# Layer 2 of a four-layer kernel: the second transposes of every odd unit move to the PSUM bank of the query products

## The reference

```
q = z @ wq @ fcq_w + fcq_b            # 16 heads of 64, likewise k and v
scores = einsum('bihd,bjhd->bhij', q, k) / scale
attn = softmax(scores, axis=-1)
out = einsum('bhij,bjhd->bihd', attn, v)
return out.reshape(b, n, 1024) @ fco_w + fco_b
```

## Time and profile before

| | us |
|---|---|
| median of three timed executions | 2760.54 |
| the profiled execution | 2755.35 |
| its span, first to last instruction | 2753.6 |
| layer 2, slots of the attention | about 1339 to 2074 |
| TensorE busy over the span | 2410.3 |
| idle of TensorE before the transposes of L2143 | 69.2 |

### The profile page before, as it was taken

How to read it: one execution, slowest core, us unless ns; L and a number is a source line. 1 busy time by engine, 2 the same in 40 slices (tenths; PEclk the granted TensorE clock), 3 DMA queues, 4 the chain that set the end, 5 groups by cost and what they waited for, 6 DMA issues and landing times.

```text
span 2753.6 us, 39485 instructions
## 1 busy us (share of the span) xinstructions
PE 2410.3 (88%) x13864; PEld 1554.8 (56%) x13864; DVE 1810.2 (66%) x3844; ACT 1306.5 (47%) x3393; POOL 1239.2 (45%) x1120
## 2 busy tenths in 40 slices
PE   6687799999999999997888999999889689897888
PEld 3475345555555555555445666665554467676766
DVE  5677576777767777664678777777656664656634
ACT  4576524344343433433355666666546324445443
POOL 2553166676776777763366333332000541333331
PEclk8899799999999999997899999999999787999999
DMA  4464300000000000002912222222101262212113
GB/s 171 143 196 137 97 1 1 1 1 1 1 1 1 1 1 1 1 1 92 222 41 66 69 71 70 70 70 77 32 1 36 60 184 50 57 44 57 34 51 100
DMA packets 189333, 158.82 MB, mean 58 GB/s; under 512 B 101408, under 2 KB 168480, under 8 KB 188320
## 3 DMA queue, kind: packets, MB, share of 16 engines
q1 hardware_dynamic: 166352, 90.25, 12.1%
q0 software_dynamic: 22784, 66.05, 7.8%
HBM read 126.49 MB, written 59.51 MB: 68 GB/s over the span
## 4 chain that ended last, share of the span: by engine, by line
PE 38%; DVE 9%; ACT 4%; issue 2%; DMA 0%; POOL 0%; SPq 0%; ACTq 0%; DVEq 0%
PE bank L65 32%; PE bank L2143 4%; DVE work L2151 2%; DVE work L2087 2%; ACT work L2113 1%; ACT L3341 1%; DVE weights_odd L3455 1%; DVE weights_odd L3457 0%; DVE work L3403 0%; ACT weights_odd L3067 0%; DVE work L2131 0%; DVE weights_even L3403 0%; DVE work L3606 0%; PE bank L3014 0%; DVE work L3455 0%
## 5 line engine op out<-in xcount | busy, mean ns | idle before, releaser
L1535 POOL TENSOR_TENSOR work<-work 128x512 f32<-128x512 f32 x384 | 489.0, 1273 | 302.3 <-DVE work L1527 282.4
L65 PE MATMUL bank<-work 64*128 64x256 f32 (+5 forms) x4384 | 589.3, 352 | 26.2 <-ACT work L3381 8.0
L65 PE MATMUL bank<-weights_odd,normed_channels 128*128 128x512 f32 (+2 forms) x1088 | 509.8, 576 | 53.1 <-DVE work L1527 52.5
L65 PEld LDWEIGHTS bank<-work 64*128 64x128 f32 (+4 forms) x4384 | 412.0, 171 | 228.9 <-issue 151.4
L2113 ACT ACTIVATE work<-bank,work 128x256 f32<-128x256 f32 x512 | 235.9, 473 | 243.3 <-DVE work L2100 238.5
L1527 DVE TENSOR_TENSOR work<-bank,work 128x512 f32<-128x512 f32 x360 | 244.7, 687 | 113.1 <-PE bank L65 101.8
L65 PEld LDWEIGHTS bank<-weights_odd,normed_channels 128*128 128x128 f32 x1088 | 175.9, 193 | 180.0 <-DVE work L1527 99.4
L1602 ACT ACTIVATE work<-bank,work 128x256 f32<-128x256 f32 x256 | 119.0, 470 | 297.1 <-DVE work L1589 296.9
L599 POOL DMA_INDIRECT weights_even<-in_L_Wx,expert_slots x112 | 113.4, 1012 | 291.4 <-PE bank L672 224.9
L2087 DVE TENSOR_REDUCE work<-bank 128x2 f32<-128x512 f32 x256 | 164.8, 685 | 119.6 <-PE bank L65 119.3
L2143 PE MATMUL bank<-constants,work 128*128 128x128 f32 x1024 | 164.9, 284 | 69.2 <-DVE work L2151 64.2
(11 more groups left out here) (355 smaller groups left out, 4211.8 us busy)
## 6 DMA issues: line engine op xcount, KB each, us to landing
filter_matrices<-in_L_filters SPq DMA_DIRECT2D x24, 512.0 KB, 7.6
work<-filter_matrices SPq DMA_DIRECT2D x16, 768.0 KB, 5.7
weights_even<-noted_rows SPq DMA_DIRECT2D x56, 132.0 KB, 2.3
noted_rows<-in_empty SPq DMA_DIRECT2D x11, 660.0 KB, 9.4
noted_rows_in<-in_empty SPq DMA_DIRECT2D x8, 660.0 KB, 9.2
weights_odd<-noted_rows_in SPq DMA_DIRECT2D x40, 132.0 KB, 2.2
work<-token_rows SPq DMA_DIRECT2D x16, 256.0 KB, 3.5
token_rows_out<-in_zeros SPq DMA_DIRECT2D x6, 640.0 KB, 19.0
```

The costliest lines, as they stand in the source:

```text
L65: return pe.matmul(out, lhsT, rhs, start=first, stop=last, skip_group_check=True)
L1535: gp.tensor_tensor(self.sum_of(p), self.sum_of(p), self.product_of(p), ALU.add).then_inc(s["l1_add"], 1)
```

## The change

The second transposes of every odd unit, and their evacuation by ScalarE, use the bank `b_misc`. Their wait on VectorE's copy of half 0 goes; in its place comes a wait for the evacuation of the latest query product. The query product waits until ScalarE has read the transposes from `b_misc`. The first transposes of an even unit wait for VectorE's copy of half 0 of the unit before, no longer for ScalarE's copy of half 1.

```
     def tensor_query(self, pe, on, n):
         s, (g, m) = self.k.sem, divmod(n, L2_PAIRS)
         on.wait_ge(s["l2_q"], n)
+        self.wait_turned_scores(on, 2 * (2 * n - 5) + 1)
         mm(pe, self.b_misc[:, :], self.Fq[:, m * P:(m + 1) * P], cols(self.k.xn, g)).then_inc(s["l2_q_mm"], 1)
...
+    def turn_bank(self, n, half):
+
+        return self.b_misc if half == 1 and n % 2 == 1 else self.b_turn
+
     def tensor_turn(self, pe, on, n, half):
-        s, h = self.k.sem, 2 * n + half
+        s, h, bank = self.k.sem, 2 * n + half, self.turn_bank(n, half)
         on.wait_ge(s["l2_p"], 2 * h + 2)
-        self.wait_turned_scores(on, h - 1)
+        if half == 1 and n % 2 == 1:
+            on.wait_ge(s["l2_q"], min((n + 5) // 2, L2_PAIRS * GROUPS))
+        elif half == 1:
+            self.wait_turned_scores(on, h - 1)
+        else:
+            self.wait_turned_scores(on, 2 * (n - 1) + (n % 2 == 1))
         for jc in range(2):
             for i in range(2):
-                last = pe.transpose(self.b_turn[:, jc * SEQ + i * P:jc * SEQ + (i + 1) * P],
+                last = pe.transpose(bank[:, jc * SEQ + i * P:jc * SEQ + (i + 1) * P],
                                     self.p[h % 6][:, i * SEQ + jc * P:i * SEQ + (jc + 1) * P], self.k.ident)
         last.then_inc(s["l2_pt_mm"], 1)
...
         on.wait_ge(s["l2_pv"], n - 1)
-        a.activation(self.pt[h % 4], self.b_turn[:, :], ACT.Copy).then_inc(s["l2_pt_act"], 1)
+        a.activation(self.pt[h % 4], self.turn_bank(n, 1)[:, :], ACT.Copy).then_inc(s["l2_pt_act"], 1)
```

## The result

The changed kernel takes 2717.2 us (median of 4 runs, 2709.2 to 2717.9) against 2761.5 us (median of 4, 2758.0 to 2763.7): a ratio of 0.983, 95% interval 0.982 to 0.985. That is 44.3 us less; forecast were 50.5 us less and 2710.0. The same kernel, timed again on two later occasions, gave 0.982 [0.980, 0.984] (2708.3 against 2760.7 us, 52.4 less) and 0.982 [0.978, 0.986] (2790.9 against 2843.1 us, 52.1 less). The kernel before itself took 2761 us on two of the four occasions and 2843 and 2839 us on the other two, so kernels are compared within one occasion, or stage by stage.

A forecast was written before the change was run, and what follows sets the result against it. The prediction took TensorE to set the pace among the expert pairs. Its terms, 33.8 + 6.5 + 3.9 + 3.7 + 4.3 - 1.7 = 50.5 us, came off 2760.54 for 2710.0 us; range 2698 to 2728.

The forecast's parts named there:

- The wait and its price: Odd second transposes: without the wait for VectorE's copy, 0.93 us less per pair of slots, 33.8 us over 36 expert pairs.
- The floor in plain slots: Eight pairs without experts or staging: VectorE and ScalarE become the bound, gain 0.43 to 0.51 us each, 3.9 in sum.
- The first slots: First five odd slots with VectorE busy routing: shorter waits at separate places, 4.3 us gained in sum.
- part (c): Even first transposes wait for a copy that ended long before: frees 2.1 us at most, taken at 0.
- Behind the experts: Slots behind the expert pairs: 6.2 us gained, 3.7 in slots with joins and 2.5 in plain pairs.
- The rows of the first pair: Slot 32: TensorE arrives before the fetched rows, whose time GpSimd's scatters set; 1.7 us given back, bounds 0 and 4.
- The added waits: Query waits for ScalarE's copy, odd half 1 for the query's evacuation with 3.3 us of cover: both cost 0.
- Nothing behind layer 2 depends on a clock of its own, so the rest moves as a block: Everything after layer 2: shifts earlier unchanged, giving 2704.9 us profiled and 2710.0 us for the median.
- Rival 1: All slots: VectorE and ScalarE bind at 0.5 us; expert pairs lose 15.5 us of gain, 2725.5 us; chance 0.12.
- rival 2: All slots: no floor, the whole 64.2 us wait for VectorE's copy comes off, 2696.3 us; chance 0.12.
- rival 3: New waits end as late as the old, or the gain is lost elsewhere: 2760 us, give or take 3; chance 0.05.
- Rival 4: Expert pairs: TensorE's clock falls to 1.2 GHz, a quarter of them giving 2801 us; chance 0.03.

The follow-up runs named there:

- e1: Changed kernel with the odd second transposes waiting again for VectorE's copy of half 0: 2845.5 us against 2843.1 for the kernel before, ratio 1.0015.
- e6: Changed kernel plus one more VectorE maximum (128x256) in every unit of layer 2: ratio 0.984 to the kernel before, layer 2 685.0 us.
- e7: Changed kernel with TensorE issuing the four second transposes of every odd unit twice: ratio 0.988 to the kernel before, layer 2 701.7 us.
- e5: Changed kernel with first transposes of even units also waiting for ScalarE's copy again: ratio 0.981 to the kernel before, layer 2 678.3 us.
- e8: Changed kernel unedited, timed and profiled again: ratio 0.982 to the kernel before, layer 2 680.3 us, layer 3 683.2 us.
- e9: Changed kernel with expert pairs and the joins behind them begun two slots later: ratio 0.981 to the kernel before, layer 2 727.7 us.
- mark 1: Label for profiled kernels run where the kernel before takes some 2761 us, as opposed to some 2840 us.
- e12: Changed kernel unedited, one more run where the kernel before takes some 2840 us: layer 2 729.2 us, layer 3 716.8 us.

## Why the prediction was right, and where it was not

Section by section, in us of layer 2, kernel before against changed. The forecast's terms are laid on the sections by where their slots lie: 7.9 is what it had for the ten pairs ahead of the first rows, 6.2 the 3.7 of the join slots and 2.5 for the plain pairs behind the experts.

| from to | before | changed | gain | forecast |
|---|---|---|---|---|
| first maxima to slot 12 | 67.08 | 61.60 | 5.48 | 4.3 |
| slots 12 to 32 | 98.48 | 89.41 | 9.07 | 7.9 |
| slot 32, the first rows | 4.66 | 5.66 | -1.00 | -1.7 |
| expert pairs | 402.58 | 370.06 | 32.52 | 33.8 |
| the rest to layer 3 | 159.44 | 154.37 | 5.07 | 6.2 |
| sum | 732.24 | 681.10 | 51.1 | 50.5 |

- **The wait and its price: right.** e1 puts back that one wait, and the whole loss comes back. The signs named ahead came near too: the clock is 1.00 in all expert pairs, a pair takes 10.29 us (10.26 expected), the idle time before its even maxima is 0.49 us (0.47); the wait for the copy is 5.0 us, at the border of the "under 5". A pair gained 402.58/36 - 370.06/36 = 0.903 us and not 0.93. The hole's end was read rightly (1.01 to 1.02 us behind the v products), but what follows the transposes starts 0.49 us behind them now and 1705.06 - 1704.59 = 0.47 before: with a hole ahead of them the four run a little denser. That is 0.02 of the 0.03, 0.7 of the 1.3 us by which the term was too high.
- **The floor in plain slots: right in kind, too low in size.** The step said that VectorE and ScalarE become the bound there and that the gain is the idle time before the even maxima, 0.43 to 0.51 us a pair. The bound is borne out: e6 and e7 both hide there, and the chain from maxima to maxima has no gap. The kernel before shows it as well. Its even plain slots ran at this floor already, 4.43 us from 2041.99 to 2046.42, its odd ones took 5.02 from 2036.97, and in the changed kernel both kinds take 4.42 to 4.43 (maxima at 1984.87, 1989.30 and 1993.72).

```profile
2036.97 1.28 DVE L2087 TENSOR_REDUCE work<-bank 128x2 f32<-128x512 f32 x2
2041.99 1.29 DVE L2087 TENSOR_REDUCE work<-bank 128x2 f32<-128x512 f32 x2 [0.50 <-PE bank L65]
2046.42 1.28 DVE L2087 TENSOR_REDUCE work<-bank 128x2 f32<-128x512 f32 x2
```

So such a pair gained 0.59 us where 0.50 of idle time stood. Some 0.08 of the difference is the view's: when maxima follow a normalisation at once they start before its row ends (in the changed kernel at 1481.65, the row ahead of them runs from 1481.09 for 0.64). The three plain pairs ahead of the experts gained 2.08 us together and not 1.4, the seven with staging 6.99 and not 6.5: the 1.2 us by which the ten pairs were too low.
- **The first slots: too low by 1.2 us.** Some 0.8 of it is part (c), which stood at 0 (e5). The rest isn't taken apart; these slots are a chain of seven with routing between, summed as five separate waits, and VectorE is at its limit there (e6: 3.6 us longer).
- **Behind the experts: 1.1 us too high, and again the clock.** The slots with joins gained what was forecast (a pair of them 17.63 to 16.72 us). But the first full slot behind ScalarE's silu grew from 5.01 to 6.85 us: TensorE waits 1.30 us for an exponential and then runs at 1.2 GHz for 6.8 us from 1918.7, four score products in 1.80 us and eight v products in 1.98 where 1.08 is usual. In e8 the same slot took 5.62.

```profile
1918.39 1.80 PE L65 MATMUL bank<-work 64*128 64x256 f32 x4 [1.30 <-ACT work L2114]
1920.13 1.12 PE L2153 MATMUL bank<-constants,work 128*128 128x128 f32 x4
1921.17 1.98 PE L65 MATMUL bank<-work 128*64 128x256 f32 x8
```

- **The rows of the first pair: right in place.** TensorE does wait in slot 32, and slot and wait were named; the size is 1.0 us of slot (1.09 of wait), not 1.7. Before, the same instruction waited for nothing at 1510.20; in e8 the wait is 1.39 us and TensorE runs at 1.2 GHz for 3.4 us from 1494.0, and slots 32 and 33 take 12.56 us together, against 10.67 in the first profile of the changed kernel and 10.57 before. The forecast of 1.7 has no term for the clock. That GpSimd's scatter sets it, still gapless at 1.27 us apart and over at 1490.5, is what the timeline shows; e9, meant to test it, could not.

```profile
1489.54 0.96 POOL L589 DMA_INDIRECT noted_rows<-work,expert_slots  x1 [0.30 <-issue]
1490.81 0.99 POOL L599 DMA_INDIRECT weights_even<-in_L_Wx,expert_slots  x1 [0.30 <-issue]
```
```profile
1494.65 0.44 PE L672 MATMUL bank<-constants,weights_even 128*128 128x128 f32 x2 [1.09 <-DMA weights_even<-noted_rows]
```

- **The added waits: right.** No wait of TensorE for the evacuation of the query product (L2065) appears, and among the experts TensorE has no idle time left at all.
- **"Nothing behind layer 2 depends on a clock of its own, so the rest moves as a block": wrong.** This is the step that failed: in the profiled execution 2704.9 us were forecast and 2717.5 came, and the 12.6 between are, but for rounding, the 15.5 of layer 3 less the 2.2 ahead of layer 2 and the 0.6 that layer 2 gained beyond the 50.5. Layer 3 came out at anything from 679.6 to 696.0 us in six profiles under mark 1, and its length goes with its time at 1.2 GHz: from 139.9 to 184.3 us low it grows by 16.4, 0.37 us for each. Ahead of the first difference the low stretches fall at the same places of layer 3 in both kernels; the first that differs, 24 us long instead of 20, begins some 212 us into it. The fences are e8 and the first profile of the changed kernel, one program, some 240 us into layer 3: the same two groups of matmuls at both levels, behind the same wait of 1.29 us.

```profile
2259.58 1.12 PE L65 MATMUL bank<-work,weights_odd 128*128 128x512 f32 x2 [1.29 <-ACT work L3376]
2260.54 1.05 PE L65 MATMUL bank<-weights_odd 128*128 128x128 f32 x8
```
```profile
2260.03 2.07 PE L65 MATMUL bank<-work,weights_odd 128*128 128x512 f32 x2 [1.29 <-ACT work L3376]
2261.90 1.80 PE L65 MATMUL bank<-weights_odd 128*128 128x128 f32 x8
```

Whole layer 3 of e8 beside the row above (695.09 us, PE 595.45, clock 0.87): the 12 us are all in TensorE's busy time, 12.75, with as many matmuls.

```profile
2018.20:2701.40 683.20, 582.70 (x4114) 440.65 (x4114) 372.05 (x801) 298.86 (x496) 208.68 (x200) 0.89 0.25 68
```

What decides at which level a stretch runs in a given run was not found. In the timed runs layers can't be told apart, so it is likely, and not shown, that the 7.2 us from 2710.0 to 2717.2 are layer 3's as well. They do vary for one and the same edit (44.3 and 52.4 us of gain), and the total time at the low level doesn't settle it: with a mean granted clock of 0.932 the changed kernel took 2709.9, 2712.9, 2717.5 and 2717.9 us.

- **The rivals.** Rival 1 (VectorE and ScalarE bind everywhere at the 0.5 us of the plain slots) is refuted by the 0.90 us that every expert pair gained and by e7, whose 0.43 us show in full there; rival 2 (no floor, 64.2 us) by the gain per pair, 0.90 and not more; rival 3 by every run of the changed kernel. Rival 4, the slower clock in the expert pairs, did not come: 1.00 in the row of 1700 to 1750. The Trainium skill's section on cycling through PSUM banks (TensorE: Matmul & The Clock Gate, A second HAM failure mode: psum-queue depth-cycling) tells of a kernel that idled in small gaps between its groups of matmuls. These rows have the banks change more often and no gap left, and the clock stayed at 1.00; no run here shows what more switching does where gaps remain.

## What to carry to other kernels

Price a wait by what the engine could start next, read from a neighbouring slot that does not have it (1.94 - 1.01 us), not by its idle time in the list; and then ask which engine is full, by adding a little work to each in turn, kind of slot by kind of slot: among the experts 0.41 us more on VectorE hid and 0.43 us more on TensorE showed in full. Where both hide, look for a chain that goes round through two engines and leaves idle time on each, as in the plain slots; work added beside the chain doesn't test it. Ask also whether the time after the change is steady where nothing was edited. Here a stage of 680 us differed by 12 us between two executions of one program and by up to 16 between kernels that don't differ in it, a third of the gain, and a single pair of profiles would have charged it to the edit; compare stage by stage, and take more than one profile.

## What the runs showed of the hardware that was not expected

Where the kernel before takes 2840 us instead of 2761, 48 us of it lie in layer 2, in both kernels; much of the rest lies in layer 3 (708.5 to 722.8 us against 679.6 to 696.0). The 48 begin at about 1412 us, just behind the start of GpSimd's indirect scatters (L589, from 1407.6 in e12), and end with them: slots of 4.43 us become 5 to 18 us long. TensorE and VectorE then stand still for long stretches without a releaser that the trace can name. Two places of e12, and its whole stretch:

```profile
1426.70 1.97 PE L65 MATMUL bank<-work 128*64 128x256 f32 x8 [8.84 <-issue]
```
```profile
1430.32 1.29 DVE L2088 TENSOR_REDUCE work<-bank 128x2 f32<-128x512 f32 x2 [12.14 <-remote]
```
```profile
1412.80:1535.00 122.20, 85.95 (x430) 47.08 (x430) 61.55 (x173) 46.52 (x158) 61.54 (x64) 0.80 0.15 46
```

TensorE is busy 86 of 122 us there, at a clock of 0.80, and the DMA engines only 0.15 of the time. In the expert pairs that follow the period is 10.29 us again. What holds the engines up is open; no run tested it. The occasions differ in the chip as well: the runs of 2761 us beside e5 to e8 were on one chip, those of 2843 and 2839 us on two others, so chip and moment can't be told apart either.
